# The last stage over sorted tokens: 43 tiles of one column each, fetched and stored row by row by GpSimd, in place of all 16 columns for every token

## The reference

```python
similarity = jnp.einsum('bsd,cd->bsc', _l2norm(x), _l2norm(col_emb))
h = jax.nn.gelu(x @ gate_w1 + gate_b1, approximate=False)
gate_values = jax.nn.sigmoid(h @ gate_w2 + gate_b2)
logits = similarity + gate_values
k = max(1, int(C * SPARSITY))
_, top_idx = jax.lax.top_k(logits, k)
mask = jnp.sum(jax.nn.one_hot(top_idx, C, dtype=logits.dtype), axis=-2)
weights = mask * jax.nn.softmax(logits, axis=-1)
cols = jax.nn.gelu(jnp.einsum('bsd,cdn->bscn', x, W_cols) + b_cols, approximate=False)
cols = cols * weights[..., None]
combined = cols.reshape(Bq, Sq, -1)
y = combined @ proj_w + proj_b + x
mu = jnp.mean(y, axis=-1, keepdims=True)
var = jnp.mean((y - mu) ** 2, axis=-1, keepdims=True)
out = (y - mu) * jax.lax.rsqrt(var + 1e-05) * ln_g + ln_b
```

## Time and profile before

| | |
|---|---|
| three timed runs | 1379.3, 1380.5, 1384.4 us (median 1380.5) |
| the profiled execution: its span, first to last instruction | 1385.6 us |
| its own time apart from the span | not given; the median of the timed runs is 5.1 us under the span |
| TensorE busy | 1304.1 us |
| VectorE, ScalarE, GpSimd busy | 968.4, 678.4, 528.1 us |
| last stage | from 1080 us to the end |
| granted TensorE clock, mean | 0.971 of full |

### The profile page before, as it was taken

How to read it: one execution, slowest core, us unless ns; L and a number is a source line. 1 busy time by engine, 2 the same in 40 slices (tenths; PEclk the granted TensorE clock), 3 DMA queues, 4 the chain that set the end, 5 groups by cost and what they waited for, 6 DMA issues and landing times. The chain is left out here.

```text
span 1385.6 us, 32665 instructions
## 1 busy us (share of the span) xinstructions
PE 1304.1 (94%) x12672; PEld 924.2 (67%) x12672; DVE 968.4 (70%) x1641; ACT 678.4 (49%) x1447; POOL 528.1 (38%) x781
## 2 busy tenths in 40 slices
PE   4789999999999985999999999999998899999996
PEld 4565777877787763666777677667775575555555
DVE  7776666567656768888888888888885553454445
ACT  5854211221122124787787778877876452232220
POOL 1428888888880008333333333333320552000000
PEclk9999999999999996999999999999999699999999
DMA  8515454545451009566655556666540000000000
GB/s 222 127 42 159 133 166 135 170 135 165 134 160 42 35 4 189 94 102 101 99 93 92 91 94 102 102 100 100 93 80 2 1 1 1 14 14 26 13 13 26
DMA packets 92814, 120.28 MB, mean 87 GB/s; under 512 B 7426, under 2 KB 78939, under 8 KB 90388
## 3 DMA queue, kind: packets, MB, share of 16 engines
q1 hardware_dynamic: 83476, 87.85, 31.9%
q0 software_dynamic: 9216, 30.73, 8.2%
HBM read 96.45 MB, written 22.10 MB: 86 GB/s over the span
## 5 line engine op out<-in xcount | busy, mean ns | idle before, releaser
L1251 DVE TENSOR_REDUCE s_neg_max<-banks 112x3 bf16<-112x1461 f32 (+1 forms) x192 | 290.2, 1511 | 45.0 <-PE banks L1367 44.8
L1165 ACT ACTIVATE s_prob<-banks 128x448 f32<-128x448 f32 x512 | 272.3, 544 | 91.6 <-PE banks L1393 76.5
L702 DVE TENSOR_TENSOR s_m<-banks,s_base 128x512 f32<-128x512 f32 x256 | 161.1, 683 | 99.2 <-PE banks L856 98.9
L1393 PE MATMUL banks<-s_q_t,s_k_t 112*128 112x112 bf16 x2048 | 186.5, 215 | 1.1 <-ACT s_prob L1165 1.0
L1393 PEld LDWEIGHTS banks<-s_q_t,s_k_t 112*128 112x128 bf16 x2048 | 124.2, 98 | 72.5 <-issue 50.5
L856 PE MATMUL banks<-s_gate_sel,s_tw 64*128 64x256 f32 x1024 | 130.8, 394 | 1.6 <-DVE s_m L702 1.5
L899 PE MATMUL banks<-s_m,s_act_t 128*112 128x256 f32 x512 | 128.2, 388 | 1.5
L1409 PE MATMUL banks<-s_prob,s_v 128*32 128x112 f32 (+1 forms) x4096 | 125.8, 263 | 0.7 <-ACT s_prob L1165 0.7
L881 PEld LDWEIGHTS banks<-s_x_t,s_m 128*128 128x128 f32 x1024 | 116.7, 192 | 10.6 <-issue 7.6
L881 PE MATMUL banks<-s_x_t,s_m 128*128 128x112 f32 x1024 | 122.4, 278 | 0.0
L1890 PE MATMUL banks<-s_proj,s_weighted 128*112 128x256 f32 x512 | 115.4, 380 | 0.0
(11 more groups left out here) (271 smaller groups left out, 2340.7 us busy)
## 6 DMA issues: line engine op xcount, KB each, us to landing
k_parts<-s_k_split POOLq DMA_DIRECT2D x64, 281.2 KB, 3.7
s_k_t<-k_parts SPq DMA_DIRECT2D x32, 562.5 KB, 7.9
s_tw<-in_tw SPq DMA_DIRECT2D x16, 1024.0 KB, 5.5
s_k_raw<-in_ctx_k POOLq DMA_DIRECT2D x64, 187.5 KB, 3.8
s_k_t<-k_parts SPq DMA_DIRECT2D x32, 375.0 KB, 5.3
s_v_raw<-in_ctx SPq DMA_DIRECT2D x32, 256.0 KB
s_src<-in_ctx SPq DMA_DIRECT2D x8, 896.0 KB, 16.2
s_k_t<-k_parts SPq DMA_DIRECT2D x32, 187.5 KB, 9.1
```

Of the source, the lines that this page charges most:

```text
L702: nc.vector.tensor_tensor(dst[:, :, :, rows_], got, base[:, :, rows_].unsqueeze(2).broadcast_to([P, 2, B, HR]), ALU.add).then_inc(S["merge ...
L1165: nc.scalar.activation(prob[t % 2][:, c, :], w.bank(SCORE + n % SRING, P, TILE), ACT.Exp, scale=DH ** -0.5).then_inc(S["exp_done"], 1)
L1251: nc.vector.tensor_reduce(neg_max[half][:, ROWS + first:ROWS + end, 0], w.banks[0:T, MAX:MAX + end - first, 0:NKEY], AX.X, ALU.max, negate ...
L1393: last = nc.tensor.matmul(w.bank(SCORE + n % SRING)[:, s * T:(s + 1) * T], k_t[k][0:ROWS_MAX, h, c * P:(c + 1) * P], q_t[k][0:ROWS_MAX, h, :],
```

## The change

The gate part stays, but for L1595, the copy into `x_t`, which falls away. While it runs, SyncE writes both biased arrays as rows of 512 numbers (`xn` beside `x_res`) into a table in HBM, `x_rows`, one row for each token; GpSimd does its 64 additions in the order of the groups.

After the winner is known, the tokens are sorted by column on the chip. A running count (`cum`) and two matmuls give each token its rank in its column; each column's count is rounded up to tiles of 128 slots. 3584 tokens in 16 columns can never need more than 43 tiles (`SLOT_TILES`), and the loop always runs over 43. 32 small matmuls with one-hot factors (`spot`, `carry`) turn the places round into a table: for each slot the token and its weight (`comes_from`, `goes_to`, `weight`), and for each tile its column (`column_of`).

Then for each of the 43 tiles: GpSimd fetches 128 rows by an indirect DMA (`fetch`), TensorE transposes them (`turn`), ScalarE reads the tile's column number into a register, copies this column's weights (`put_weights`), the rows (`evacuate_row`) and takes the GELU of two matmuls (`column`); TensorE reads the number as well and projects with one matmul (`output`); VectorE weights, adds and normalises; GpSimd stores 128 rows by an indirect DMA to their places in the result (`store`; slots without a token are addressed out of bounds and not written). The layer norm's square root is taken for 8 tiles together. Since more semaphores are needed than are free, those of stage 1 are cleared by GpSimd at the end of stage 3 and used again.

```diff
-                        nc.scalar.activation(x_t[:, :, b * T:(b + 1) * T], got, ACT.Copy)
...
+                for g in range(NG):
+                    rows_ = slice(g * GB, (g + 1) * GB)
+                    wait(sp, "x_biased", GB * (g + 1))
+                    sp.dma_start(rows_of[:, rows_, D:2 * D], w.x_res[:, rows_, :]).then_inc(rows_in, 16)
+                    wait(sp, "kept", GB * (g + 1))
+                    sp.dma_start(rows_of[:, rows_, 0:D], xn[:, rows_, :]).then_inc(rows_in, 16)
...
+                def fetch(n):
+                    if n >= SEMS:
+                        pool.wait_ge(row_in[n % SEMS], 16 * (n // SEMS))
+                    if n >= RING4:
+                        pool.wait_ge(stored[n % SEMS], 16 * ((n - RING4) // SEMS + 1))
+                    nc.gpsimd.indirect_dma_start(row(n), None, w.x_rows[:, :],
+                                                 bass.IndirectOffsetOnAxis(ap=comes_from[:, n:n + 1], axis=0))\
+                        .then_inc(row_in[n % SEMS], 16)
+                def store(n):
+                    wait(pool, "res_done", n + 1)
+                    if n >= SEMS:
+                        pool.wait_ge(stored[n % SEMS], 16 * (n // SEMS))
+                    nc.gpsimd.indirect_dma_start(out_rows, bass.IndirectOffsetOnAxis(ap=goes_to[:, n:n + 1], axis=0), y_of(n),
+                                                 None, bounds_check=B * T - 1, oob_is_err=False)\
+                        .then_inc(stored[n % SEMS], 16)
+                for n in range(AHEAD4):
+                    fetch(n)
+                for n in range(N_TILES + LAG):
+                    if n + AHEAD4 < N_TILES:
+                        fetch(n + AHEAD4)
+                    if n >= LAG:
+                        store(n - LAG)
...
+                def load_columns_of(n):
+                    return act.value_load(column_of[0:1, n:n + 1], min_val=0, max_val=C4 - 1)
+                def put_weights(n, c):
+                    wait(act, "col_ps", n - 1)
+                    nc.scalar.activation(w_tile[n % 2][:], w_cols[:, :, bass.ds(c * N4, N4)], ACT.Copy).then_inc(S["w_done"], 1)
+                for n in range(N_TILES):
+                    if n + 1 < N_TILES:
+                        c_next = load_columns_of(n + 1)
+                        put_weights(n + 1, c_next)
+                        evacuate_row(n + 1)
+                    gelu(n, c)
...
+                for n in range(N_TILES + LAG):
+                    now, old = n < N_TILES, n >= LAG
+                    if now:
+                        summed(n)
+                    if old:
+                        centred(n - LAG)
+                    if now:
+                        stat(n)
+                    if old:
+                        finish(n - LAG)
+                    if now:
+                        mean_variance(n)
...
+                def output(n):
+                    c = pe.value_load(column_of[0:1, n:n + 1], min_val=0, max_val=C4 - 1)
+                    wait(pe, "gelu_done", n + 1)
+                    wait(pe, "summed", n - 3)
+                    nc.tensor.matmul(w.bank(4 + n % 4, P, D), hid_c[n % 2][:], proj[:, bass.ds(c * D, D)],
+                                     start=True, stop=True).then_inc(S["y_ps"], 1)
+                for n in range(N_TILES):
+                    if n + 1 < N_TILES:
+                        turn(n + 1)
+                    column(n)
+                    if n >= 1:
+                        output(n - 1)
```

More of the change, by code:

```diff
@@ L1088, in _ @@
                     at(b + 3, put_values)
+                for signal in w.finished:
+                    pool.sem_clear(signal)
             @block.scalar
@@ new lines, in stage4 @@
+        slot = sb("s4_slot", [T, C4, B])
+        pos, tile_of, within = (sb("s4_" + n, [T, B]) for n in ("pos", "tile_of", "within"))
+        in_tile = sb("s4_in_tile", [T, B, N_TILES])
+        carry = sb("s4_carry", [T, B, 2, N_TILES])
+        spot = sb("s4_spot", [T, B, P])
+        pad = sb("s4_pad", [P, N_TILES])
+        goes_to = sb("s4_goes_to", [P, N_TILES], I32)
+        comes_from = sb("s4_comes_from", [P, N_TILES], I32)
+        weight = sb("s4_weight", [P, N_TILES])
+        past = sb("s4_past", [1, N_TILES, C4])
@@ L1844, in weights @@
-                def weights(g):
-                    if g == 0:
-                        wait(pe, "wts_done", 1)
-                    wait(pe, "wts_odd" if g % 2 else "wts_even", g // 2)
-                    for r in range(GB):
-                        last = nc.tensor.matmul(w.bank(2 + g % 2)[0:3 * C4, r * T:(r + 1) * T],
-                                                parts[:, GB * g + r, :, :].rearrange("t n c -> t (n c)"), ident16[:],
-                                                start=True, stop=True)
-                    last.then_inc(S["wts_ps"], 1)
@@ L1865, in _ @@
[L1865 to L1882 removed]
+                wait(pe, "cum_done", 1)
@@ new lines, in _ @@
+                nc.tensor.matmul(w.bank(1, P, C4), ones16[:], cum[:, :, B - 1], start=True, stop=True)
+                nc.tensor.matmul(w.bank(0, T, C4 * B), not_before[:], hit[:].rearrange("t c b -> t (c b)"), start=True, stop=False)
+                nc.tensor.matmul(w.bank(0, T, C4 * B), ones16[:, 0:T], cum[:].rearrange("t c b -> t (c b)"), start=False,
+                                 stop=True).then_inc(S["rank_ps"], 1)
+                wait(pe, "token_done", 1)
+                for b in range(B):
+                    if b % 8 == 0:
+                        wait(pe, "spot_done", b // 8 + (2 if b else 2))
+                    last = nc.tensor.matmul(w.bank(1)[:, 2 * C4:2 * C4 + 2 * N_TILES], spot[:, b, :],
+                                            carry[:, b, :, :].rearrange("t k n -> t (k n)"),
+                                            start=(b == 0), stop=(b == B - 1))
```

436 lines of the change are left out of this document (214 added, 222 removed).

## The result

The changed kernel takes 1322.9 us (median of four runs, 1322.1 to 1325.2), the kernel before 1382.5 in the same session: a ratio of 0.957, 95% interval 0.954 to 0.959, about 60 us. The profiled execution of the changed kernel has a span of 1321.7 us and a time of 1323.45. The forecast was 1310.

The account below looks back on a forecast made before the run. TensorE was taken to bound the last stage's column part. First tile at 1173, 42 periods of 3.0 us and a 16 us end gave span 1315, time 1310 us; range 1270 to 1368, with 0.5 on 1289 to 1331.

Parts of the forecast that it names:

- Gate part, 0 us: Last stage's gate part: TensorE bounds it and its rows stay, so losing 32 ScalarE copies changes nothing, 0 us.
- cover: Gate part: routing, lasting until 1164, hides GpSimd's 64 additions (48 us, to about 1140) and the last stores behind them.
- Routing: New steps on the path, from last logits at 1132.6 to slots known at 1164.5; first tile ready for VectorE at 1173.
- Eight tiles at 3.9 and the rest at 2.8: Loop: period in us, with TensorE at the lower clock for eight tiles, then the higher; p = 3.0 on average.
- rival 1: Loop: TensorE stays at the lower clock throughout, period 3.9 us, span 1353, time 1348; chance 0.2.
- GpSimd: Loop: two indexed DMAs per tile at 1.2 us each, 2.4 us a tile.
- Rivals 2 and 3: Loop: GpSimd bounds it at 2.0 us per DMA, time 1360 (0.15); or waits for landing or handles indices singly, 1499 (0.12).
- The estimate of 11 us: Loop, GpSimd's indexed DMA: 128 index reads at about 102 cycles each and 1.2 GHz.
- ScalarE: Loop: 2.4 us a tile (1.7 to 3.0), of which 0.7 us for the register load.
- The end: After tile 42's sum: statistics, root and inverse 5 us, nine tiles finished 7 us, last store 4 us; 16 us.
- The time: Whole kernel: span 1315 us, less 5.1 us from profiled span to timed median, gives 1310 us.
- theory A: For unread matmuls in routing only: clock rises and holds, table 7.0 us, loop period 2.56 us by GpSimd, time about 1306.

Follow-up runs that it names:

- fewer_adds: The changed kernel without GpSimd's additions for the last four images (8 of 64): 1319.9 us, ratio 0.954 to the kernel before.
- routing_edits: Changed kernel with GpSimd's 64 additions merged into 16, hits written in memory order, and GpSimd's half of the carry moved to VectorE: 1328.5 us.
- one_filler: Changed kernel plus unread matmuls in routing and one per loop tile, fetches 18 ahead, hits in memory order, carry on VectorE, short tail: 1283.9 us.
- one_column: Changed kernel with column 0's weights as a constant for every tile, so both register loads are gone: 1323.7 us, ratio 0.957 to the kernel before.
- heat_routing: Changed kernel with 120 unread bf16 matmuls filling TensorE's idle spots from the last logits to the first fetched tile: 1304.1 us.
- heat_loop: Changed kernel with three unread bf16 matmuls per tile in the loop only, and three banks for the sums instead of four: 1317.3 us.
- no_loop_filler: Changed kernel plus unread matmuls until the first tile, none in loop; fetches 18 ahead, hits in memory order, carry on VectorE, short tail: 1295.2 us.

## Why the prediction was right, and where it was not

Sign and size came out, and the cause that it gave, the columns that are no longer computed, is the right one: from the last logits to the end it took 253.0 us and now takes 1321.7 - 1131.1 = 190.6. That the number came so near is in part luck: the sum hides errors that cancel.

- **Gate part, 0 us:** it took 52.5 us before (from the stage's first VectorE instruction at 1080.1 to 1132.6) and 48.3 after (1082.9 to 1131.1), 4.2 less; the logits came only 1.5 early because the stage began 2.8 later in this execution. TensorE has 1.00 at 1100 to 1105, where the earlier trace rows shows 0.50; whether the 32 copies that are gone brought this about was not tested. GpSimd's additions were costed only as "cover" for their stores. That they hold VectorE was no step at all: 5.26 - 0.69 = 4.6 us on the path, shown by fewer_adds.
- **Routing:** 6.8 us late. 4.6 are the held addition; the hits 1.7 (2.38 for the 0.69 that the winner's row of before stood for), which is the order of writing, by routing_edits 1.4 of them. `spot` and GpSimd's half of `carry` were put beside each other, beside the earlier trace rows, with the table waiting for GpSimd. But `spot` is held while GpSimd computes, and the table waited for VectorE's own half of `carry` behind it (L1829): the first `spot` took 1.22 instead of 3.52 when VectorE did both halves, and the table began 0.8 us earlier behind `in_tile`, 4.5 for 5.3. The early logits give 1.5 back. Another 1.9 us come between the slots and the first sum (10.4 us for the 8.5 forecast). The table's low clock was forecast rightly: 13.9 us, and 7.35 in one_filler at the high one.
- **The clock in the loop:** this step failed. "Eight tiles at 3.9 and the rest at 2.8" took it from the earlier trace rows that a busy TensorE rises within some tiles. It never rose; rival 1 (0.2) is what happened, at another price. Its 3.9 had 0.7 us for a register load, 0.3 around it and a division by 0.86 from the earlier trace rows; one_column shows that the load costs nothing, and no such factor is in the rows, where TensorE counts as busy for all of 25 us. Its 2.3 us of matmuls and transposes became 2.81 with the gaps between the pieces. The period of 2.78 instead of 3.0 takes 42 x 0.22 = 9 us from the forecast, almost what the late first tile adds, 8.8; that the two cancel is luck.
- **GpSimd:** 0.98 and 1.01 us for an indexed DMA instead of 1.2, with 0.30 to the next: 2.6 us a tile, near the 2.4 of the forecast and just under TensorE's 2.81, so hidden here. Rivals 2 and 3 fall: the first fetch occupies GpSimd for 1.08 us, not until its rows land (3.6 us in the median of the 43). The estimate of 11 us by the GPSIMD page of the Trainium skill ("GPSIMD Engine Reference", Performance pitfalls for Q7 kernels) is off by a factor of ten here.
- **ScalarE:** the register load is 0.28 us, against 0.7. The floor of about 600 ns that the Trainium skill gives ("DMA: Bandwidth & Descriptors", Latency and other measured facts) is twice this; the measurement decides.
- **The end:** 22.8 us instead of 16. VectorE is done 10.7 us after the last sum (12 forecast). That GpSimd's stores, one each 1.3 us, finish another 3.8 later was no term, and the end behind the last one was costed as 4 us where 8.4 were (3.6 behind the last store of before; what fills the rest is open).
- **The time:** the 12.9 us between 1310 and 1322.9 are 6.7 of span and 6.2 of conversion. The forecast took 5.1 us off the span, but in every run on record the time is 1.7 to 2.0 us above the span of the same execution. So the profiled execution of before (1385.6, about 1387 of time) was a long one against the medians of 1380.5 to 1385.3, and the 5.1 held for it alone; the changed kernel's median lies 1.2 above its profiled span.

## What to carry to other kernels

When work is taken from a TensorE that was dense, ask what clock the rest will run at: here less work ran at half speed for the whole loop, and one filler per tile (1295.2 to 1283.9 us) was worth more than any edit tried on the work itself. An engine that is "off the path" is only so until it shares something with one that is on it: GpSimd's additions were hidden as time, and still held VectorE, in the gate part and in the routing, worse when they were merged into fewer, longer ones. And a time that fits a theory is not enough: heat_routing met theory A's number by way of two periods, neither of them A's.

## What the runs showed of the hardware

- A TensorE that counts as busy all the time can stay at 1.2 GHz: 25.00 of 25 us at 0.50, stretch after stretch, with gaps of 0.33 and 0.65 us in the weight load's rows between pieces. It rose when fillers were added (heat_loop) and held with one or three per tile. Without any it fell behind a wait of 1.85 us in heat_routing and of 1.11 us in no_loop_filler, and stayed up behind one of 1.11 us in heat_routing; what decides is open. The Trainium skill ("TensorE: Matmul & The Clock Gate", What's actually happening) says that the throttled state is the default and that activity releases it; the rise in heat_loop agrees, while the changed kernel's loop, busy by the profile for 25.00 of 25 us, was not released.
- VectorE's addition with both operands in SBUF was held by GpSimd's: 5.26 us against 0.69. The Trainium skill ("SBUF — State Buffer", Who interferes with whom) says that such an instruction contends with a GpSimd instruction that reads SBUF. The trace agrees, and shows for how long: VectorE's row starts at 1131.89 and ends only after GpSimd's last addition, seven instructions on. So these two engines meet at SBUF as well as at semaphores.
- Writing 512 bf16 numbers with a stride took 2.38 us; reading the f32 operand with a stride and writing in order took 1.01.
